# Two attention layers with experts on one core: where the product with the values stands in a slot, and where three weight loads are issued

## The chip, the cores and the metric

The kernel runs on one core of a Trainium2 chip. A core has five engines, each with a queue of its own that it works off in order: TensorE (PE, matrix products; its weight loads are listed apart as PEld), VectorE (DVE), ScalarE (ACT), GpSimd (POOL) and SyncE (SP), which here only issues transfers. They meet by semaphores. The metric is the device time of one launch in microseconds (us), lower is better.

## What is computed

Four sequences of 512 tokens with 128 features run through two layers. Cut to what matters:

```python
x = L0_attn_x                                   # (4, 512, 128), f32
xn = layernorm(x)
x = x + attention_0(xn) + swiglu_0(xn)          # 16 heads of 8; hidden 384, int weights / 127
xn = layernorm(x)
x = x + attention_1(xn, block_mask) + experts_1(xn)
# attention: softmax(q k^T / sqrt(8)) v, then a projection; the second one has a block mask
# experts: router -> best 2 of 8, capacity 1.25 * T / 8; each expert silu(x Wg) * (x Wu) @ Wd
```

## The kernel before

**Units and slots.** The work is eight units: four sequences in layer 0 (units 0 to 3), then the same four in layer 1 (units 4 to 7). A unit has 16 slots. A slot handles one block of 128 keys for four heads: two pairs of score products (`score_mms`, line 747; each pair is two products on the two halves of the array's rows), whose results ScalarE exponentiates (`exponential`, line 962) into `PT`, and one product with the values (`value_mms`, line 763, 4 products in f32 that the trace lists as 8 rows), one slot late: slot t does the product for slot t-1.

**Maxima.** Softmax needs the row maxima first. They are made 24 pairs ahead: a slot also has up to two pairs of score products for maxima (`max_mms`, line 732), which VectorE reduces (`read_max`, line 1114). There are 256 such pairs; 24 come before unit 0, so 116 slots carry two each, the last of them slot 3 of unit 7. The maxima are split (GpSimd), transposed (PE, line 739), copied to `mT` (ScalarE, line 955) and sent into rows of `QO` by SyncE (`max_rows`, line 444), for the slots 0 to 7 and 8 to 15 of a unit apart.

**PSUM.** Banks 0 to 5 form three pairs of banks. Scores, maxima, gate products and expert products take them in turn (`take_pair`): a job waits until the job three places before it in that row has been read. In a slot with maxima and nothing else the row is: score pair 0, maxima 0, score pair 1, maxima 1. So maxima 1 waits for the exponential of score pair 0 of the same slot, maxima 0 of the next slot for the exponential of score pair 1, and each score pair for VectorE's reduction of an earlier maximum. Bank 6 collects the product with the values, bank 7 is for everything else.

**Side work.** At the end of a slot PE does what is due besides: gate and up products of layer 0 (slots 9 to 11 of units 0 to 3, lines 785 and 786), expert work (two jobs a slot from slot 4 of unit 6 on, lines 792, 802, 803, 810), and `side_mms`: transposes (lines 687, 771, 777, 739), projections (line 693 and, for the values, 699 or 704), router and rank products. In slot 6 the projection of the output of the unit before is in two halves (`out_mms`, lines 822 and 825): the first between score pair 0 and score pair 1, the second at the slot's end. The first waits until `mT` was copied, since both use bank 7.

**ScalarE's row.** In each slot: exponential of pair 0, then most of the copies, then the exponential of pair 1, then `output_copy` (slots 0 and 8, line 968) or the tanh of gates (line 978) or an expert's result (line 994). `exponential` e waits for the product with the values of two slots before (`pv_done`), since `PT` has four buffers.

**SyncE's row.** Everything above issues from one queue, written out by hand: first loads, row constants, then `loads` (line 1370), the last three of which are the experts' weights `eg`, `eu` and `ed` of 1 MB each; then `sync_unit` for each unit. `loads` all count on one semaphore, `loaded`, on which the mask table (GpSimd, unit 0) and the expert products wait.

Of the kernel before, what the change touches and what calls it, by code (L numbers as in the profile page):

```python
# [12 lines left out]
P = 128  # L13
# [4 lines left out]
def build(nc, x, wq, wk, wv, bq, bk, bv, wo, bo, wg_T, wu_T, wd_T, src_blocks, tgt_blocks, router_T, eg_T, eu_T,  # L18
# [33 lines left out]
    with ExitStack() as ctx:  # L52
# [3 lines left out]
        def sem(name):  # L56
            return ctx.enter_context(nc.semaphore(name))
# [20 lines left out]
        w_router = sb("w_router", [P, E])  # L78
# [88 lines left out]
        emptied = sem("emptied")  # L167
        empty_ready = sem("empty_ready")
        loaded = sem("loaded")
        x_loaded = [sem(f"x_loaded{b}") for b in range(B)]  # L170
        zeros = sem("zeros")
        consts = sem("consts")
# [84 lines left out]
        def layer(u):  # L257
            return u // B
# [129 lines left out]
        def operand_writes(sp, p, side):  # L388
            if p >= 2 and side == 0:
                sp.wait_ge(qk_rows[(p - 2) % 3], reads_of(p - 2))  # L390
                if p == 2:
                    for landed in first_rows:
                        sp.wait_ge(landed, 16 * 4)
            for i in range(3):
                sp.wait_ge(part_ready[side], 3 * p + i + 1)
                a, z, step = SLOTS[i][side]
                dst = z_dram[p % 2][side].rearrange("s m t -> m s t")[:, a:z:step, :]
                n = len(range(a, z, step))
                sp.dma_start(dst, part[i][:, side, :].unsqueeze(1).to_broadcast([P, n, S])).then_inc(
                    z_written[side], 16)  # L400
# [46 lines left out]
        def sync_unit(sp, u):  # L447
            p, n = u + 2, u + 1
            if u == U - 2:
                for e in range(2):  # L450
                    load_places(sp, e)
                load_meta(sp)
                for e in range(2, 4):
                    load_places(sp, e)
            max_rows(sp, u, 1)
            if p < U:
                operand_writes(sp, p, 0)
                operand_writes(sp, p, 1)
                if layer(p) == 0:
                    operand_reads_0(sp, p)  # L460
                else:
                    operand_reads_1(sp, p, 0)
            if u == U - 2:
                for e in range(4, 7):
                    load_places(sp, e)
            if n < U:
                max_rows(sp, n, 0)
            if u == U - 2:
                load_places(sp, 7)
            if p < U and layer(p) == 1:  # L470
                operand_reads_1(sp, p, 1)
            if u < 2:
                empty_places(sp, u)
# [321 lines left out]
        def gate_up_1(pe, g):  # L795

            e, i, c = g // 4, g % 4 // 2, g % 2
            pe.wait_ge(loaded, N_LOAD)
            pe.wait_ge(places_ready, e + 1)
            pair = take_pair(pe, "gate1", g)  # L800
            cols, x_T = slice(i * P, (i + 1) * P), places_T[e % 2][:, c * HALF:(c + 1) * HALF]
            pe.matmul(ps[:, 2 * pair, 0:HALF], eg[:, e, cols], x_T, start=True, stop=True).then_inc(gate_ps[1], 1)  # L802
            pe.matmul(ps[:, 2 * pair + 1, 0:HALF], eu[:, e, cols], x_T, start=True, stop=True).then_inc(up_ps[1], 1)  # L803
# [95 lines left out]
        def tensor_unit(pe, u):  # L899
            if u < 3:  # L900
                pe.wait_ge(rows_set[u], 16 * N_ROW_DMAS)
            pe.wait_ge(m_rows[0], 16 * M_DMAS * (u + 1))
            for slot in range(SLOTS_U):
                if slot == 8:
                    pe.wait_ge(m_rows[1], 16 * M_DMAS * (u + 1))
                maxima = pairs_at(u, slot)
                score_mms(pe, u, slot, 0)
                if maxima:
                    max_mms(pe, maxima[0])
                if u > 0 or slot > 0:  # L910
                    value_mms(pe, SLOTS_U * u + slot - 1)
                if slot == 6 and u >= 1:
                    pe.wait_ge(mT_ready, 2 * u + 2)
                    out_mms(pe, u - 1, (0, 1))
                score_mms(pe, u, slot, 1)
                if maxima:
                    max_mms(pe, maxima[1])
                if gate_at(u, slot) is not None:
                    gate_up_0(pe, gate_at(u, slot))
                for kind, n in expert_work_at(u, slot):  # L920
                    if kind == "places":
                        places_mms(pe, n)
                    elif kind == "gate1":
                        gate_up_1(pe, n)
                    else:
                        expert_out(pe, n)
                side_mms(pe, u, slot)
# [282 lines left out]
        def last_vector(dve):  # L1210
            normalize_out(dve, U - 1, 1)
            for b in range(B):
# [13 lines left out]
                 (w_v[1][:], wv[1]),  # L1226
                 *((b_v1[32 * c:32 * c + 32], bv[1][None, 32 * c:32 * c + 32].to_broadcast([32, 32])) for c in range(4)),
                 (w_proj[1][:], wo[1]), (b_proj[1][:], bo[1][None, :].to_broadcast([P, D])),
                 (w_router[:], router_T), (eg[:], eg_T), (eu[:], eu_T),
                 (ed[:], ed_T.rearrange("e (b p) d -> p e b d", p=P))]  # L1230
        N_LOAD, N_FIRST = 16 * len(loads), 16 * len(first_loads)

        def load_x(sp, b):
            sp.dma_start(xs[b][:], x[b].rearrange("(t p) d -> p t d", p=P)).then_inc(x_loaded[b], 16)
# [276 lines left out]
```

## Time and profile before

| | us |
|---|---|
| median of 3 runs | 543.98 (542.29 to 545.46) |
| profiled execution, device time | 544.03 |
| its span (first to last instruction) | 542.0 |
| PE busy | 454.8 (84%) |
| VectorE busy | 400.5 (74%) |
| ScalarE busy | 328.8 (61%) |
| GpSimd busy | 262.5 (48%) |
| mean granted clock of TensorE | 0.95 of 2.4 GHz |

The device time is the span and 2.0 us around it. PE is the busiest engine and has 53% of the chain that ended last; VectorE has 18%, ScalarE 10%. PE idles 87.2 us in all, of which 26.9 us lie before unit 0 begins at 49.96 us and 17.1 us behind 513.55 us, in the last four slots and the end.

Two products of a pair run on different rows of the array at once, so a pair of score products shows 0.39 us while the next one may start 0.22 us after it.

### The profile page before, as it was taken

Reading aid. Unit: us, or ns where it says so; the run is one execution under the profiler, and the core shown is the slowest. Engines: PE = TensorE matmul, PEld = TensorE weight load, DVE = VectorE, ACT = ScalarE, POOL = GpSimd, SP = SyncE. Lnnn points to the kernel's source line nnn. Section 1 sums busy time; section 2 is a strip of 40 time slices with the busy share of each in tenths; the row PEclk is TensorE's granted clock in tenths of the full one; section 3 lists DMA queues with packets and bytes.
Section 4 is the critical chain, followed back from the end, with each engine's and each line's share of the span. In section 5 each row is a group of like instructions: output and inputs, shape, how many; then the busy total and the mean of one; then the engine's idle time right before and its main releaser. Section 6 shows DMA issues by size and latency. Waiting matters only on the chain.

```text
span 542.0 us, 9302 instructions
## 1 busy us (share of the span) xinstructions
PE 454.8 (84%) x3394; PEld 169.4 (31%) x3394; DVE 400.5 (74%) x538; ACT 328.8 (61%) x422; POOL 262.5 (48%) x499
## 2 busy tenths in 40 slices
PE   3456979889988999899989898987899999999952
PEld 1101213224322433242312431221245453455511
DVE  5699778886998699869887798789876777623204
ACT  2102666776677667656676577777766567667560
POOL 6861263724425562886378657884201233163240
PEclk9755889999999999999999999999999999999995
DMA  3896596244511360626252645174731111010018
GB/s 82 238 230 89 89 343 106 93 163 146 90 43 61 118 62 4 66 72 127 25 52 39 157 43 56 41 160 68 109 52 32 45 50 50 4 44 25 21 47 219
DMA packets 143742, 48.27 MB, mean 89 GB/s; under 512 B 109890, under 2 KB 139090, under 8 KB 142866
## 3 DMA queue, kind: packets, MB, share of 16 engines
q1 hardware_dynamic: 141394, 42.93, 38.1%
q0 software_dynamic: 2304, 4.76, 2.6%
q8 instruction: 27, 0.44, 0.3%
q14 instruction: 17, 0.14, 0.1%
HBM read 22.81 MB, written 23.14 MB: 85 GB/s over the span
## 4 chain that ended last, share of the span: by engine, by line
PE 53%; DVE 18%; issue 10%; ACT 10%; DMA 4%; SPq 4%; POOL 1%; POOLq 0%; ACTq 0%; DVEq 0%
PE ps L763 14%; DVE mx L1114 11%; PE ps L747 9%; PE ps L732 7%; ACT PT L962 6%; PE ps L802 3%; PE ps L810 3%; PE ps L785 2%; PE ps L803 2%; SPq L433 2%; PE ps L693 2%; PE ps L825 2%; PE ps L822 2%; PE ps L786 1%; DVE th L1135 1%
## 5 line engine op out<-in xcount | busy, mean ns | idle before, releaser
L1114 DVE TENSOR_REDUCE mx<-ps 128x2 f32<-128x1024 f32 x256 | 309.4, 1223 | 73.1 <-PE ps L732 65.1
L962 ACT ACTIVATE PT<-ps 128x1024 f32<-128x1024 f32 x256 | 258.6, 1026 | 125.9 <-PE ps L747 116.5
L763 PE MATMUL ps<-PT,Vp 128*32 128x512 f32 x1024 | 138.1, 611 | 5.4 <-ACT PT L962 4.4
L732 PE MATMUL ps<-KO,QO 48*128 48x512 bf16 (+1 forms) x512 | 104.5, 406 | 39.7 <-ACT PT L962 22.6
L747 PE MATMUL ps<-QO,KO 59*128 59x512 bf16 x512 | 100.2, 390 | 3.8 <-DMA QO<-mT 2.5
L520 POOL DMA_INDIRECT y_tokens<-expert_io,meta x40 | 38.6, 964 | 71.5 <-ACT expert_io L994 48.5
L747 PEld LDWEIGHTS ps<-QO,KO 59*128 59x128 bf16 x512 | 24.6, 93 | 142.8 <-issue 87.9
L1135 DVE SCALAR_TENSOR_TENSOR th<-th,ps 128x320 f32<-128x320 f32 (+1 forms) x44 | 23.8, 541 | 35.2 <-ACT th L978 29.4
L732 PEld LDWEIGHTS ps<-KO,QO 48*128 48x128 bf16 (+1 forms) x512 | 25.6, 96 | 70.9 <-ACT PT L962 38.6
L545 POOL CAST mp<-mx 128x32 bf16<-128x32 f32 x16 | 3.4, 214 | 82.9 <-DVE mx L1114 78.7
L509 POOL DMA_INDIRECT x_places<-xe,place_i x32 | 31.9, 995 | 22.3 <-ACT PT L962 15.2
L763 PEld LDWEIGHTS ps<-PT,Vp 128*32 128x32 f32 x1024 | 20.4, 108 | 45.7 <-issue 39.7
L978 ACT ACTIVATE th<-ps 128x320 f32<-128x320 f32 (+1 forms) x44 | 21.1, 487 | 12.0 <-PE ps L802 5.8
L802 PE MATMUL ps<-expert_io,eg 128*128 128x320 f32 x64 | 24.4, 462 | 2.1 <-ACT expert_io L994 0.6
L1150 DVE SCALAR_TENSOR_TENSOR h_all<-th,ps 128x320 f32<-128x320 f32 (+1 forms) x44 | 23.8, 541 | 1.5
L955 ACT COPY mT<-ps 24x512 bf16<-24x512 bf16 x16 | 9.0, 562 | 26.1 <-PE ps L739 26.1
L492 POOL TENSOR_SCALAR xe<-xs,mv,rstd 128x128 f32<-128x128 f32 x28 | 22.2, 802 | 0.8
L994 ACT ACTIVATE expert_io<-ps,meta 128x128 f32<-128x128 f32 x40 | 11.2, 372 | 18.6 <-PE ps L810 18.6
L803 PE MATMUL ps<-expert_io,eu 128*128 128x320 f32 x64 | 22.4, 432 | 0.0
L810 PE MATMUL ps<-ed,h_all 128*128 128x128 f32 x160 | 19.4, 276 | 1.2 <-DVE h_all L1150 1.2
L810 PEld LDWEIGHTS ps<-ed,h_all 128*128 128x128 f32 x160 | 18.9, 192 | 3.0 <-DVE h_all L1150 1.7
L1120 DVE RECIPROCAL rden<-ps 128x32 f32<-128x32 f32 x16 | 5.6, 349 | 16.3 <-PE ps L771 16.3
(166 smaller groups left out, 475.1 us busy)
## 6 DMA issues: line engine op xcount, KB each, us to landing
z<-part SPq DMA_DIRECT2D x16, 384.0 KB
z<-part SPq DMA_DIRECT2D x16, 256.0 KB
QO<-z SPq DMA_DIRECT2D x64, 48.0 KB
KO<-z SPq DMA_DIRECT2D x64, 48.0 KB
x_places<-expert_io SPq DMA_DIRECT2D x2, 1300.0 KB, 7.4
expert_io<-x_places SPq DMA_DIRECT2D x8, 320.0 KB, 3.5
QO<-z SPq DMA_DIRECT2D x6, 384.0 KB
KO<-z SPq DMA_DIRECT2D x6, 384.0 KB
```

The lines of the kernel that those rows point to most:

```text
L509: pool.indirect_dma_start(out=x_places[:], out_offset=bass.IndirectOffsetOnAxis(ap=place_i[:, b, t, k:k + 1], axis=0), in_=xe[p % 2][:, t, ...
L520: pool.indirect_dma_start(out=y_tokens[:], out_offset=bass.IndirectOffsetOnAxis(ap=meta[:].bitcast(I32)[:, e, j, 0:1], axis=0), in_=y_sb[e ...
L732: mm = pe.matmul(ps[:, 2 * pair + half, :], rows_of(QO[u % 3], half, 2 * s + jj, rows, (qt, qt + 1)), rows_of(KO[u % 3], half, 2 * s + jj, ...
L747: mm = pe.matmul(ps[:, 2 * pair + half, :], rows_of(KO[u % 3], half, 2 * s + jj, ROWS, (k, k + 1)), rows_of(QO[u % 3], half, 2 * s + jj, R ...
L763: last = pe.matmul(ps[32 * g:32 * g + 32, PV_BANK, :], Vp[u % 2][:, k, head(s, g), :], PT[:, (2 * t + g % 2) % 4, g // 2, :], start=(s % 2 ...
L802: pe.matmul(ps[:, 2 * pair, 0:HALF], eg[:, e, cols], x_T, start=True, stop=True).then_inc(gate_ps[1], 1)
L803: pe.matmul(ps[:, 2 * pair + 1, 0:HALF], eu[:, e, cols], x_T, start=True, stop=True).then_inc(up_ps[1], 1)
L810: last = pe.matmul(across(pair, j * P, (j + 1) * P), h1_T[:, e % 2, i, j * P:(j + 1) * P], ed[:, e, i, :], start=(i == 0), stop=(i == EB - 1))
L962: act.activation(PT[:, e % 4], ps[:, 2 * pair:2 * pair + 2, :], ACT.Exp).then_inc(exp_done, 1)
L1114: dve.tensor_reduce(mx[:, a, qt, col:col + 5:4], ps[:, 2 * pair:2 * pair + 2, :], AX_X, ALU.max, negate=True).then_inc(max_read, 1)
L1135: dve.scalar_tensor_tensor(out=t, in0=t, scalar=1.0, in1=ps[:, bank, 0:n], op0=ALU.add, op1=ALU.mult).then_inc(gate_done[L], 1)
L1150: dve.scalar_tensor_tensor(out=dst, in0=t, scalar=0.5, in1=ps[:, bank + 1, 0:n], op0=ALU.mult, op1=ALU.mult).then_inc(h_ready[L], 1)
```

## The change

Two things. In `tensor_unit`, the product with the values moves from between maxima 0 and score pair 1 to behind maxima 1, ahead of the gate, expert and side work. Where a slot has no maxima it moves behind score pair 1. Nothing else in PE's row moves, and no other engine's row but SyncE's. In SyncE's row, the loads of `eg` and `eu` move from the end of the first loads to unit 0, behind the rows for its second half and the operand writes for unit 2; the load of `ed` moves to the same place in unit 1. They get a semaphore of their own, on which the expert products now wait.

```diff
@@ sync_unit
                 operand_writes(sp, p, 0)
                 operand_writes(sp, p, 1)
+                if u < 2:
+                    for dst, src in expert_loads[0:2] if u == 0 else expert_loads[2:3]:
+                        sp.dma_start(dst, src).then_inc(experts_loaded, 16)
                 if layer(p) == 0:
                     operand_reads_0(sp, p)
@@ gate_up_1
-            pe.wait_ge(loaded, N_LOAD)
+            pe.wait_ge(experts_loaded, N_EXPERT)
@@ tensor_unit
                 score_mms(pe, u, slot, 0)
                 if maxima:
                     max_mms(pe, maxima[0])
-                if u > 0 or slot > 0:
-                    value_mms(pe, SLOTS_U * u + slot - 1)
                 if slot == 6 and u >= 1:
                     pe.wait_ge(mT_ready, 2 * u + 2)
                     out_mms(pe, u - 1, (0, 1))
                 score_mms(pe, u, slot, 1)
                 if maxima:
                     max_mms(pe, maxima[1])
+                if u > 0 or slot > 0:
+                    value_mms(pe, SLOTS_U * u + slot - 1)
                 if gate_at(u, slot) is not None:
                     gate_up_0(pe, gate_at(u, slot))
@@ loads
-                 (w_router[:], router_T), (eg[:], eg_T), (eu[:], eu_T),
-                 (ed[:], ed_T.rearrange("e (b p) d -> p e b d", p=P))]
+                 (w_router[:], router_T)]
+        expert_loads = [(eg[:], eg_T), (eu[:], eu_T), (ed[:], ed_T.rearrange("e (b p) d -> p e b d", p=P))]
```

PE's row in slot 4 of unit 2, which ends with a key projection as side work. L747 are score pairs, L732 maxima, L763 the product with the values; `exp_done` is a wait for an exponential, `max_read` for a reduction. Before:

```order
L747 MATMUL ps<-QO,KO 128x512 [waits max_read]
L747 MATMUL ps<-QO,KO 128x512
L732 MATMUL ps<-KO,QO 128x512 [waits exp_done]
L732 MATMUL ps<-KO,QO 128x512
L763 MATMUL ps<-PT,Vp 32x512 [waits exp_done]
L763 MATMUL ps<-PT,Vp 32x512 x3
L747 MATMUL ps<-QO,KO 128x512 [waits max_read]
L747 MATMUL ps<-QO,KO 128x512
L732 MATMUL ps<-KO,QO 128x512 [waits exp_done]
L732 MATMUL ps<-KO,QO 128x512
L693 MATMUL ps<-xnT,w_k 128x512 [waits xnT_ready,onT_ready,qk_f_ready]
```

The same slot in the changed kernel, whose lines are numbered 4 higher (L751 scores, L736 maxima, L767 values, L697 projection):

```order
L751 MATMUL ps<-QO,KO 128x512 [waits max_read]
L751 MATMUL ps<-QO,KO 128x512
L736 MATMUL ps<-KO,QO 128x512 [waits exp_done]
L736 MATMUL ps<-KO,QO 128x512
L751 MATMUL ps<-QO,KO 128x512 [waits max_read]
L751 MATMUL ps<-QO,KO 128x512
L736 MATMUL ps<-KO,QO 128x512 [waits exp_done]
L736 MATMUL ps<-KO,QO 128x512
L767 MATMUL ps<-PT,Vp 32x512 [waits exp_done]
L767 MATMUL ps<-PT,Vp 32x512 x3
L697 MATMUL ps<-xnT,w_k 128x512 [waits xnT_ready,onT_ready,qk_f_ready]
```

Between score pair 0 and maxima 1, which waits for that pair's exponential, the product with the values stood before; now only maxima 0 and score pair 1 do. The value product stands between maxima 1 and the side work.

PE's row in slot 6 of unit 3, from score pair 0 to the second half of the output projection. Before:

```order
L747 MATMUL ps<-QO,KO 128x512 [waits max_read]
L747 MATMUL ps<-QO,KO 128x512
L732 MATMUL ps<-KO,QO 128x512 [waits exp_done]
L732 MATMUL ps<-KO,QO 128x512
L763 MATMUL ps<-PT,Vp 32x512 [waits exp_done]
L763 MATMUL ps<-PT,Vp 32x512 x3
L822 MATMUL ps<-w_proj,o_T 128x128 [waits h_ready0,onT_ready,mT_ready]
L825 MATMUL ps<-wd,h_all 128x128 x3
```

In the changed kernel:

```order
L751 MATMUL ps<-QO,KO 128x512 [waits max_read]
L751 MATMUL ps<-QO,KO 128x512
L736 MATMUL ps<-KO,QO 128x512 [waits exp_done]
L736 MATMUL ps<-KO,QO 128x512
L826 MATMUL ps<-w_proj,o_T 128x128 [waits h_ready0,onT_ready,mT_ready]
L829 MATMUL ps<-wd,h_all 128x128 x3
```

The value product went from ahead of the wait for `mT` to behind score pair 1 and maxima 1.

SyncE's row at the start of unit 0 in the changed kernel; L445 are the maxima rows, L400 the operand writes for unit 2, L411 its operand reads:

```order
L1374 DMA w_router<-in_router_T 128x8
L445 DMA QO<-mT 3x4x512 x2
L400 DMA z_0<-part 128x3x512
L400 DMA z_0<-part 128x2x512
L400 DMA z_0<-part 128x512
L400 DMA z_1<-part 128x3x512
L400 DMA z_1<-part 128x2x512
L400 DMA z_1<-part 128x512
L462 DMA eg<-in_eg_T 128x2048
L462 DMA eu<-in_eu_T 128x2048
L411 DMA QO<-z_0 48x4096
```

Before, `eg`, `eu` and `ed` stood between `w_router` and the maxima rows. Now `eg` and `eu` are behind the operand writes, ahead of the operand reads of unit 2.

## Rows read from the trace of the kernel before

**Rows 1.** Windows, units 0 to 7: length, busy PE PEld DVE ACT POOL, clock, DMA, GB/s

```profile
49.96:105.93 55.97, 48.71 (x292) 12.62 (x293) 46.11 (x52) 36.30 (x42) 25.04 (x56) 0.90 0.57 139
105.93:161.74 55.81, 51.23 (x346) 17.49 (x345) 46.50 (x57) 38.07 (x45) 19.76 (x41) 1.00 0.42 120
161.74:217.53 55.79, 51.51 (x348) 17.55 (x346) 46.51 (x57) 38.31 (x46) 29.39 (x68) 1.00 0.30 66
217.53:275.17 57.64, 52.20 (x468) 18.21 (x466) 46.90 (x63) 38.23 (x46) 37.56 (x76) 1.00 0.43 69
275.17:328.51 53.34, 47.24 (x456) 16.34 (x454) 43.03 (x57) 36.32 (x43) 37.53 (x76) 1.00 0.46 74
328.51:377.97 49.46, 42.92 (x420) 12.12 (x419) 41.62 (x47) 35.72 (x41) 36.77 (x71) 1.00 0.51 85
377.97:452.17 74.20, 69.02 (x564) 31.88 (x563) 56.91 (x78) 49.55 (x74) 17.75 (x25) 1.00 0.31 57
452.17:513.55 61.38, 57.59 (x365) 31.58 (x365) 27.85 (x49) 39.65 (x68) 20.30 (x25) 1.00 0.09 30
```

**Rows 2.** Timeline of PE and ACT, a quiet slot: start, length, operation [idle before]

```profile
106.96 0.39 PE L732 MATMUL ps<-KO,QO 48*128 48x512 bf16 x2 [0.63 <-ACT PT L962]
107.28 1.07 PE L763 MATMUL ps<-PT,Vp 128*32 128x512 f32 x8
108.28 0.39 PE L747 MATMUL ps<-QO,KO 59*128 59x512 bf16 x2
108.50 0.38 PE L732 MATMUL ps<-KO,QO 48*128 48x512 bf16 x2
...
109.79 0.39 PE L732 MATMUL ps<-KO,QO 48*128 48x512 bf16 x2 [0.69 <-ACT PT L962]
...
108.71 1.02 ACT L962 ACTIVATE PT<-ps 128x1024 f32<-128x1024 f32 x1 [0.89 <-PE ps L747]
```

**Rows 3.** Timeline of PE, unit 2: a slot's begin, then one with a projection

```profile
168.23 0.39 PE L747 MATMUL ps<-QO,KO 59*128 59x512 bf16 x2
168.62 0.39 PE L732 MATMUL ps<-KO,QO 48*128 48x512 bf16 x2
...
176.85 0.38 PE L732 MATMUL ps<-KO,QO 48*128 48x512 bf16 x2
177.16 1.13 PE L693 MATMUL ps<-xnT,w_k 128*128 128x512 f32 x2
178.22 0.39 PE L747 MATMUL ps<-QO,KO 59*128 59x512 bf16 x2
```

**Rows 4.** Timeline, slot 6 of unit 3, engines as named

```profile
237.35 0.39 PE L747 MATMUL ps<-QO,KO 59*128 59x512 bf16 x2
...
238.74 0.56 ACT L955 COPY mT<-ps 24x512 bf16<-24x512 bf16 x1
...
239.36 0.49 PE L822 MATMUL ps<-w_proj,o_T 128*128 128x128 f32 x2
```

**Rows 5.** Waits of PE over the whole span: in total, times, longest

```profile
PE ps L732 <- ACT PT L962: 22.6, 40, 0.8
```

**Rows 6.** Timeline of SP and PE, the start of slot 8 of unit 0

```profile
71.42 2.67 SPq L444 DMA_DIRECT2D QO<-mT  x2
...
77.39 0.39 PE L747 MATMUL ps<-QO,KO 59*128 59x512 bf16 x2 [2.55 <-DMA QO<-mT]
...
77.97 1.93 PE L763 MATMUL ps<-PT,Vp 128*32 128x512 f32 x8
```

**Rows 7.** Timeline of PE and ACT, unit 6, the slot behind an expert's output

```profile
447.02 0.39 PE L747 MATMUL ps<-QO,KO 59*128 59x512 bf16 x2
...
449.50 0.39 PE L732 MATMUL ps<-KO,QO 56*128 56x512 bf16 x2 [0.53 <-ACT PT L962]
...
447.12 1.40 ACT L994 ACTIVATE expert_io<-ps,meta 128x128 f32<-128x128 f32 x5 [2.33 <-PE ps L810]
```

**Rows 8.** Timeline of POOL, the first of the last seven sends of expert results

```profile
516.24 0.96 POOL L520 DMA_INDIRECT y_tokens<-expert_io,meta  x1 [5.31 <-ACT PT L962]
```

More of the change, by code:

```diff
@@ L169, in build @@
         loaded = sem("loaded")
+        experts_loaded = sem("experts_loaded")
         x_loaded = [sem(f"x_loaded{b}") for b in range(B)]
@@ L1228, in build @@
                  (w_proj[1][:], wo[1]), (b_proj[1][:], bo[1][None, :].to_broadcast([P, D])),
-                 (w_router[:], router_T), (eg[:], eg_T), (eu[:], eu_T),
-                 (ed[:], ed_T.rearrange("e (b p) d -> p e b d", p=P))]
-        N_LOAD, N_FIRST = 16 * len(loads), 16 * len(first_loads)
+                 (w_router[:], router_T)]
+        expert_loads = [(eg[:], eg_T), (eu[:], eu_T), (ed[:], ed_T.rearrange("e (b p) d -> p e b d", p=P))]
+        N_LOAD, N_EXPERT, N_FIRST = 16 * len(loads), 16 * len(expert_loads), 16 * len(first_loads)
         def load_x(sp, b):
```

## The prediction

> **What bounds the kernel now.** I read first the busy time of each unit, then PE's timeline slot by slot, then its waits. In units 1 to 7 PE is busy 87 to 94% of the time [rows 1], so it is the engine that sets the pace, but not everywhere. Two kinds of slot must be told apart, and the reader should see them in the timeline.
>
> A quiet slot has two score pairs, two pairs of maxima and the product with the values, and nothing else. There PE waits. From one maxima 0 to the next [rows 2]: the value product starts 0.32 us later, score pair 1 1.00 us after that, its exponential 0.43 us later and takes 1.02 us, and 0.06 us on the next maxima 0 starts, since it needs the banks that this exponential reads: 0.32 + 1.00 + 0.43 + 1.02 + 0.06 = 2.83 us, which is 109.79 - 106.96. PE idles 0.63 to 0.69 us of it. So a quiet slot is bound by a ring through PE and ScalarE.
>
> A slot with side work is bound by PE alone. Without waits, PE's own pitches are 0.22 (score pair 0), 0.32 (maxima 0), 1.00 (values), 0.22 (score pair 1) and 0.31 (maxima 1, followed by something of another kind), 2.07 us in all, plus the side work. In the slot with the key projection maxima 1 to the next score pair is 1.37 us = 0.31 + 1.06 [rows 3], so the slot takes 3.13 us, and the next maxima 0 finds its exponential done: the side work stands in the time in which PE would have waited. That is how most waits are hidden now, and PE's waits of maxima for exponentials add up to only 22.6 us in 40 places [rows 5].
>
> **The value product moved, slot by slot.** Two rings run through each slot: score pair 0 and its exponential to maxima 1 of the same slot, and score pair 1 and its exponential to maxima 0 of the next slot. Before, the first had the value product inside it (0.22 + 0.32 + 1.00 + 0.22 = 1.76 us of PE work from score pair 0 to maxima 1, against 0.43 + 1.02 + 0.06 = 1.51 us that the exponential needs), and the second had the side work. So each had its cover. Now both covers are in the second ring. In the first there are score pair 0, maxima 0 and score pair 1: 0.22 + 0.22 + 0.39 = 0.83 us until PE is empty, then 0.68 us of idling until 1.51.
>
> - *Quiet slot, after:* 1.51 (score pair 0 to maxima 1) + 0.32 + 1.00 = 2.83 us. The same as now: the wait goes from maxima 0 to maxima 1. Nothing won, nothing lost.
> - *Slot with side work s, after:* 2.83 + s, against 2.07 + s. It costs 0.76 us, of which 0.68 is idling. It can't be hidden by the side work, since that comes behind the wait.
>
> I count 116 slots with maxima. Slot 6 of units 1 to 6 is apart, which leaves 110: 81 with side work (9, 11, 12, 12, 11, 9, 13 and 4 in units 0 to 7) and 29 quiet ones.
>
> Slot 6: the first half of the output projection waits for `mT`, whose copy is behind the exponential of score pair 0. It starts 2.01 us after score pair 0 [rows 4]; the value product lies inside that. After, the start is the same 2.01 us, PE has 0.22 + 0.38 = 0.60 us of work in it and idles 1.4 us, and the value product's 1.00 us comes later. In units 1 to 7, where there is such a projection, that is 1.4 us of idling each, 9.8 us in the sum below; maxima 1 then has no wait.
>
> Behind an expert's output ScalarE first copies the result, 1.40 us [rows 7], then does the exponential of score pair 0, and maxima 1 starts 2.48 us after score pair 0 (449.50 against 447.02), still waiting for ScalarE although the value product stands before it. Against 1.51 that is 0.97 more in four such slots with maxima: 3.9 us.
>
> **The loads moved.** In unit 0 PE stands still for 2.55 us at slot 8 for the maxima rows, issued at 71.42 behind 3 MB of weights, and runs the next value product in 1.93 instead of 1.07 us [rows 2, 6]. Without the loads ahead of it that wait has between nothing and 2.5 us left; I take nothing, as two slots, 5.66 us, lie between the copy's slot and the wait. That is 2.5 us, and 0.9 for the product at the lower clock. The new places cost nothing: the issues stand behind operand writes for unit 2 that PE needs only from slot 4 of unit 1, over ten slots later, so 2 MB ahead of the operand reads (and `ed` ahead of those for unit 3) are covered; without that cover it would be again 2.5 us at a time. The mask table's loads come earlier, which nobody waits for.
>
> **The sum**, by PE's time. Busy in units 0 to 7: 48.7 + 51.2 + 51.5 + 52.2 + 47.2 + 42.9 + 69.0 + 57.6 = 420.3 us [rows 1], less 0.9 for the clock. Idling and transitions that the new order makes: 81 x 0.76 = 61.6, 29 x 0.69 = 20.0 (already there in some, but not in busy time), slot 6 9.8, experts 3.9. Waits that stay: 3.8 in unit 7 (61.38 - 57.59), where slots 4 to 15 have no maxima and the value product's place changes no ring, and some 1.5 of unit 0's first slots (of 7.3 in all, between nothing and 4.7 without the 2.55). Together 520.0 us, against 463.6 now (513.55 - 49.96): +56.4. All other present waits of PE in these units (the reductions, the normalized output) fall behind the value product and are gone in this sum.
>
> From that comes off what counts as busy but is a wait: where maxima 0 follows 0.39 instead of 0.22 us behind its score pair, as at 168.23 [rows 3], no idle time shows, because the rows overlap. PE's timeline has 77 late followers of this kind; 48 of them are not in quiet slots, each some 0.15 us: -7. The head before 49.96 is untouched. The tail isn't moved by PE: the last seven sends of GpSimd start at 516.24 [rows 8] behind an exponential that follows an expert's result copy, and the end hangs on them; quiet slots of unit 7 may get shorter by some tenths and win nothing. So **+49 us: 544 + 49 = 593 us**, from the profiled execution's 544.03, which the median of 543.98 equals.
>
> **A rule against the change.** At full clock the quiet slots of rows 2 idle 0.69 us each, and the granted clock is 1.00 in units 1 to 7 [rows 1]; after the 2.55 us wait it was at the lower level (1.93 us for a value product) [rows 6]. The Trainium skill, TensorE: Matmul & The Clock Gate, "A second HAM failure mode: psum-queue depth-cycling", tells of a kernel that went round its PSUM banks, made PE idle briefly between groups, and had its clock swing between both levels. By that rule the new waits would cost more than their length; it is a rival below. The trace speaks against it so far, with 0.69 us idling in slot after slot at 1.00.
>
> **Rivals.**
>
> 1. *The clock falls.* The longest new waits are slot 6's 1.4 us. If each sent the clock to 1.2 GHz for a slot, as the 2.55 us did, it would cost some 0.9 us for the value product and as much for the rest: 7 x 1.8 = 13 us more, 606 us; if also slots with 0.68 us did, far more (0.9 us per value product in half of 110 slots, 50 us: 643). For it: more idling than now. Against it: rows 1 and 2, as told. Chance 0.08.
> 2. *The loss is smaller, since other engines pace the side-work slots.* VectorE is busy 81 to 84% in units 1 to 5 [rows 1]. Where a gate's two products on VectorE or the reductions already hold PE, the new idling takes the place of that waiting. If a third more of the 61.6 us fell on such places, it would be 573 us. For it: units 0 to 5 idle 4 to 7 us each now. Against it: those waits are already out of the sum. Chance 0.08.
> 3. *Faster.* The mechanism: only the old waits vanish (22.6 at maxima 0, 3.4 at the load) and maxima 1 doesn't wait, because its exponential is early enough: 544 - 26 = 518 us. It decides at the point where PE has 1.51 us of work between score pair 0 and maxima 1; it has 0.83. The banks would have to be taken in another turn than the row says. Chance 0.02.
> 4. *Nothing changes but the load.* If the side work slipped into the wait after all, as it does now, every slot would be like the quiet one: 541 us, the 3.4 us won. PE works its row in order, which speaks against it. Chance 0.02.
>
> **How the numbers follow.** The forecast, 593 us with its own 580 to 603, has 0.80. Its low end is slot pitches by hand, 63.1 us for unit 2 instead of 64.1, and rival 2 in part; its high end the sum without the 7 us and with the load's 2.5 us back. For 8 in 10, with a little of rivals 1 and 2: 578 to 605. Faster by over 0.5% (2.7 us, about what a measurement of this kernel can tell from no change) 0.03, within 0.5% 0.02, slower 0.95.
>
> **What would show it.** Right: maxima rows waiting for exponentials in over 100 places, about 0.68 us each, some 75 us in all, now at the second pair of maxima; the slot with the key projection 3.9 instead of 3.1 us; unit 2 about 63 to 64 us, unit 7 only 3 to 5 us longer; the output projection in slot 6 behind 1.4 us of idling; no wait for `QO<-mT` at slot 8 of unit 0; the clock at 1.00 in units 1 to 6. Wrong: side-work slots of their old length, or value products at 1.93 us in the middle of the run.

## The result, and the profile after

The changed kernel takes 584.01 us (median of 4 runs, 583.26 to 587.78), beside 544.16 us for the kernel before on the same chip (4 runs): a ratio of 1.0749, 95% interval 1.0693 to 1.0805. It is 40 us slower, where 49 were forecast; 584 lies inside the forecast's own range of 580 to 603.

The profiled execution took 583.26 us, with a span of 580.8 us against 542.0. PE is busy 452.5 us (78%), where it was 454.8 (84%), so all of the new time is idling. PE's share of the chain that ended last rose from 53 to 58%, ScalarE's from 10 to 20%.

Windows of the changed kernel, units 0 to 7 in the first eight rows, then the last four slots of unit 7 and the end, which the row of unit 7 leaves out as [rows 1] does (length, then busy time of PE, PEld, DVE, ACT and POOL, granted clock, DMA share, GB/s):

```profile
49.83:107.46 57.63, 47.38 (x292) 13.32 (x292) 46.69 (x53) 36.76 (x42) 26.33 (x61) 0.94 0.49 120
107.46:169.97 62.51, 51.17 (x349) 18.11 (x346) 46.48 (x58) 37.26 (x44) 19.12 (x38) 1.00 0.44 125
169.97:232.64 62.67, 51.33 (x350) 18.22 (x347) 46.58 (x58) 37.43 (x45) 29.30 (x68) 1.00 0.27 55
232.64:295.71 63.07, 51.73 (x470) 18.84 (x467) 46.96 (x64) 37.43 (x45) 37.43 (x76) 1.00 0.39 63
295.71:353.21 57.50, 45.87 (x458) 16.64 (x454) 42.96 (x58) 35.64 (x42) 37.38 (x76) 1.00 0.43 68
353.21:406.65 53.44, 42.01 (x423) 12.62 (x420) 41.54 (x48) 35.52 (x40) 36.22 (x69) 1.00 0.47 79
406.65:488.40 81.75, 69.46 (x565) 32.49 (x561) 56.05 (x78) 48.33 (x73) 17.53 (x24) 1.00 0.28 52
488.40:552.42 64.02, 57.21 (x364) 31.36 (x363) 27.68 (x49) 39.57 (x68) 20.10 (x24) 1.00 0.08 27
552.42:580.80 28.38, 11.93 (x73) 4.53 (x72) 6.89 (x12) 10.30 (x15) 6.70 (x7) 0.73 0.46 127
```

Set against [rows 1], the eight units are 1.7, 6.7, 6.9, 5.4, 4.2, 4.0, 7.6 and 2.6 us longer, 39.0 in all. The head (49.83 against 49.96) and the last stretch (28.38 against 28.45) hardly changed. Unit 0, which has the load's gain in it, and unit 7, where the maxima end with slot 3, lose least; unit 6, with maxima and expert work in its slots, most. PE idles 86.4 us in the units (the lengths less the busy times) where it was 43.2. The clock stands at 1.00 from unit 1 to 7.

The waits of PE in the changed kernel (what waited, for whom, total us, times, longest):

```profile
PE ps L736 <- ACT PT L966: 57.4, 92, 0.9
PE ps L736 <- DVE mx L1118: 10.8, 21, 0.6
PE ps L826 <- ACT mT L959: 9.7, 7, 1.6
PE ps L751 <- DVE h_all L1154: 8.6, 19, 0.7
...
PE ps L751 <- DVE mx L1118: 3.6, 7, 0.7
...
PE ps L751 <- ACT expert_io L998: 2.4, 3, 0.9
```

The first row answers to [rows 5]: 57.4 us in 92 places where it was 22.6 in 40. The second is not new: it stands in the trace of before with the same 10.8 us in 21 places, all but one of them ahead of unit 0. The two rows on L751 with `h_all` and `expert_io` are score pairs that wait for a gate product's reader or for an expert result's copy.

PE's timeline in unit 2 of the changed kernel, from the second pair of scores of slot 4 to the value product of slot 6; 190.61 is score pair 0 of slot 6, 194.56 its score pair 1 (start, length, operation, idle before it and its releaser):

```profile
184.15 0.38 PE L751 MATMUL ps<-QO,KO 59*128 59x512 bf16 x2
185.21 0.39 PE L736 MATMUL ps<-KO,QO 48*128 48x512 bf16 x2 [0.68 <-ACT PT L966]
185.53 1.07 PE L767 MATMUL ps<-PT,Vp 128*32 128x512 f32 x8
186.53 1.13 PE L697 MATMUL ps<-xnT,w_k 128*128 128x512 f32 x2
187.58 0.39 PE L751 MATMUL ps<-QO,KO 59*128 59x512 bf16 x2
...
190.61 0.39 PE L751 MATMUL ps<-QO,KO 59*128 59x512 bf16 x2
...
192.58 0.49 PE L826 MATMUL ps<-w_proj,o_T 128*128 128x128 f32 x2 [1.35 <-ACT mT L959]
192.90 0.83 PE L829 MATMUL ps<-wd,h_all 128*128 128x128 f32 x6
...
194.56 0.39 PE L751 MATMUL ps<-QO,KO 59*128 59x512 bf16 x2
...
195.10 1.06 PE L767 MATMUL ps<-PT,Vp 128*32 128x512 f32 x8
```

This is the mechanism in three readings. At 185.21 the second maxima wait 0.68 us for the exponential of score pair 0. Behind them stand the value product (1.00 us) and the key projection (1.05 us), which could have filled that wait and come too late for it. And in slot 6 the projection starts 1.97 us after score pair 0 (192.58 against 190.61), as it did before [rows 4], but now with 1.35 us of idling in front, and the value product still to come at 195.10.

ScalarE in the same slot 6: the copy of `mT`, which releases the projection, stands right behind the exponential.

```profile
191.04 1.02 ACT L966 ACTIVATE PT<-ps 128x1024 f32<-128x1024 f32 x1 [0.52 <-PE ps L751]
191.97 0.56 ACT L959 COPY mT<-ps 24x512 bf16<-24x512 bf16 x1
```

### The profile page after: what moved, and what is told of

Its sections match the earlier page's. It is cut to its first block, busy times and chain, and to the rows that moved or that the text cites. A ratio compares the mean times of both kernels' runs of the same rounds, so it can differ in the third digit from the quotient of the medians.

```text
span 580.8 us, 9302 instructions
## 1 busy us (share of the span) xinstructions
PE 452.5 (78%) x3394; PEld 174.6 (30%) x3394; DVE 400.1 (69%) x538; ACT 324.2 (56%) x422; POOL 261.6 (45%) x499
## 4 chain that ended last, share of the span: by engine, by line
PE 58%; ACT 20%; DVE 10%; issue 7%; DMA 2%; POOL 1%; SPq 1%; POOLq 0%; ACTq 0%; DVEq 0%
PE ps L767 20%; ACT PT L966 16%; PE ps L736 7%; PE ps L751 7%; DVE mx L1118 5%; PE ps L814 3%; PE ps L806 3%; PE ps L807 2%; PE ps L789 2%; PE ps L697 2%; PE ps L829 2%; PE ps L826 2%; DMA h_all<-y_tokens 1%; PE ps L790 1%; DVE th L1139 1%
## 5 line engine op out<-in xcount | busy, mean ns | idle before, releaser
L966 ACT ACTIVATE PT<-ps 128x1024 f32<-128x1024 f32 x256 | 254.9, 1027 | 132.5 <-PE ps L751 124.0
L736 PE MATMUL ps<-KO,QO 48*128 48x512 bf16 (+1 forms) x512 | 104.5, 406 | 73.7 <-ACT PT L966 57.4
L767 PE MATMUL ps<-PT,Vp 128*32 128x512 f32 x1024 | 137.1, 607 | 1.7 <-issue 1.0
L751 PE MATMUL ps<-QO,KO 59*128 59x512 bf16 x512 | 98.4, 387 | 16.8 <-DVE h_all L1154 8.6
L736 PEld LDWEIGHTS ps<-KO,QO 48*128 48x128 bf16 (+1 forms) x512 | 25.2, 95 | 127.0 <-ACT PT L966 97.5
L751 PEld LDWEIGHTS ps<-QO,KO 59*128 59x128 bf16 x512 | 24.2, 93 | 100.7 <-issue 33.5
L767 PEld LDWEIGHTS ps<-PT,Vp 128*32 128x32 f32 x1024 | 20.2, 108 | 34.9 <-issue 33.1
L826 PE MATMUL ps<-w_proj,o_T 128*128 128x128 f32 x64 | 13.1, 314 | 10.9 <-ACT mT L959 9.7
```

Of the source, the lines that this page charges most:

```text
L736: mm = pe.matmul(ps[:, 2 * pair + half, :], rows_of(QO[u % 3], half, 2 * s + jj, rows, (qt, qt + 1)), rows_of(KO[u % 3], half, 2 * s + jj, ...
L751: mm = pe.matmul(ps[:, 2 * pair + half, :], rows_of(KO[u % 3], half, 2 * s + jj, ROWS, (k, k + 1)), rows_of(QO[u % 3], half, 2 * s + jj, R ...
L767: last = pe.matmul(ps[32 * g:32 * g + 32, PV_BANK, :], Vp[u % 2][:, k, head(s, g), :], PT[:, (2 * t + g % 2) % 4, g // 2, :], start=(s % 2 ...
L826: last = pe.matmul(ps[:, SIDE, tok], o_T[:, tok], w_proj[L][:], start=True, stop=(L == 1))
L966: act.activation(PT[:, e % 4], ps[:, 2 * pair:2 * pair + 2, :], ACT.Exp).then_inc(exp_done, 1)
```

## The experiments

The kernels ran in groups, each beside the kernel before. That measured 539.4 us in the first group (values alone, the loads alone for the first time, slot 6, early side work) and 543.8 to 544.3 us in the others, so each ratio is against the kernel before of its own group. The changed kernel, run again in the last group, gave 583.95 us, ratio 1.0732 [1.0706, 1.0757], with units within 0.6 us of those above. It was not run in the first group.

### The two parts apart

Values alone, the loads left in their old place (against the kernel before):

```diff
                 if maxima:
                     max_mms(pe, maxima[0])
-                if u > 0 or slot > 0:
-                    value_mms(pe, SLOTS_U * u + slot - 1)
...
                 if maxima:
                     max_mms(pe, maxima[1])
+                if u > 0 or slot > 0:
+                    value_mms(pe, SLOTS_U * u + slot - 1)
```

> The value product at its new place, all loads at their old one. My theory (the exponential of score pair 0 has lost its cover, 0.68 us of idling before maxima 1 in every slot with side work): nearly the whole loss, and the stall of unit 0 at slot 8 as before or a little less, since that slot comes later: 584 to 588 us. Rival (the loads' new place costs part of the 40 us, for instance operand reads behind 2 MB): under 575 us.

It measured 583.45 us, ratio 1.0811 [1.0768, 1.0855], span 580.5. Units 1 to 6 are 62.52, 62.67, 62.88, 57.35, 53.10 and 81.76 us, those of the changed kernel within 0.4 us. The whole loss is the value product's. The issue of the maxima rows and the start of slot 8 of unit 0, timelines of SyncE and PE of this kernel:

```profile
74.09 1.62 SPq L444 DMA_DIRECT2D QO<-mT  x2
...
78.07 0.39 PE L747 MATMUL ps<-QO,KO 59*128 59x512 bf16 x2 [0.20 <-DMA QO<-mT]
```

Against 2.55 us in [rows 6] only 0.20 us of the wait for the maxima rows is left although the loads stand ahead of them. The expectation, a stall as before or a little less, missed this. The late value products put the copy of `mT` off, so that the rows are issued at 74.09 instead of 71.42, while the first of the three weight loads is issued at nearly the same time (65.37, before 65.00). From their issue to the score pair it takes 3.98 us instead of 5.97. PE's own work in that stretch grew by less, from 3.42 to 3.78 us.

Loads alone (against the changed kernel, the value product put back between maxima 0 and score pair 1):

```diff
                 if maxima:
                     max_mms(pe, maxima[0])
+                if u > 0 or slot > 0:
+                    value_mms(pe, SLOTS_U * u + slot - 1)
...
                     max_mms(pe, maxima[1])
-                if u > 0 or slot > 0:
-                    value_mms(pe, SLOTS_U * u + slot - 1)
```

> The value product at its old place, the loads at their new one. My theory: the stall of 2.55 us at slot 8 of unit 0 and the slow clock behind it vanish, all else as before: 540 to 541 us. Rival (the loads collide with unit 2's operands): 544 us or more, with a wait of PE for a transfer of z in unit 1.

It measured 535.92 us, ratio 0.9937 [0.9921, 0.9954]. Run again in the last group it gave 541.54, ratio 0.9949 [0.9935, 0.9962]:

> The loads alone again, beside the kernel with late value products in unit 7. My theory: 0.992 to 0.995 of the kernel before. Rival (the gain of the first time was the chip's): above 0.998.

Both say some 3 us, as worked out: slots 7 and 8 of unit 0 take 2.87 and 3.97 us instead of 5.54 and 4.70 in the kernel before. At slot 8 the score pair no longer waits, and the value product runs in 1.07 us; PE's timeline of the first of the two kernels, slot 8 of unit 0:

```profile
75.87 0.39 PE L751 MATMUL ps<-QO,KO 59*128 59x512 bf16 x2
76.89 0.39 PE L736 MATMUL ps<-KO,QO 48*128 48x512 bf16 x2 [0.63 <-ACT PT L966]
77.21 1.07 PE L767 MATMUL ps<-PT,Vp 128*32 128x512 f32 x8
```

So in time the parts don't add up. Alone, the loads' new place is worth 3 us. With late value products the traces leave it some 0.3: slot 7 of unit 0 takes 3.09 us in the kernel with the values alone and 2.83 in the changed one, and of the slots behind it only five differ, by 1.3 us together and in the other direction (slot 8 of units 3 to 5 and slots 5 and 10 of unit 7). The ratios seem to say otherwise, 1.0811 against 1.0749 and 1.0732, as if the loads had won 3 to 4 us here too. But they stand on kernels before of 539.4 us and of 544.2 and 544.3; the kernels themselves took 583.5, 584.0 and 584.0.

### Slot 6

The value product of slot 6 of units 1 to 7 put back ahead of the wait for `mT`, all else as changed:

```diff
+                if slot == 6 and u >= 1:
+                    value_mms(pe, SLOTS_U * u + slot - 1)
                 if slot == 6 and u >= 1:
                     pe.wait_ge(mT_ready, 2 * u + 2)
...
-                if u > 0 or slot > 0:
+                if (u > 0 or slot > 0) and not (slot == 6 and u >= 1):
                     value_mms(pe, SLOTS_U * u + slot - 1)
```

> The changed kernel with slot 6 of units 1 to 7 in the old order (values ahead of the output projection). My theory: the value product fills the wait for mT again, 1.0 us in each of seven units, 577 us; slot 6 of unit 2 falls from 7.47 to 6.47 us. Rival (the time in slot 6 is given back later, since VectorE catches up there): less than half of that.

It measured 576.07 us, ratio 1.0673 [1.0635, 1.0712], span 573.3, which is 7.5 us below the changed kernel's: 1.0 us for each of the seven projections. The slot takes 6.47 us instead of 7.47, its length before. The waits of PE in this kernel have 2.7 us where the changed kernel has 9.7:

```profile
PE ps L826 <- ACT mT L961: 2.7, 7, 0.6
```

### Half an exponential

Four kernels leave out half of one exponential in each slot from slot 2 of unit 0 on (it then takes 0.60 instead of 1.02 us, and the results are not right): that of score pair 0 or that of score pair 1, in the changed kernel and in the kernel before. If the ring through pair 0 sets the changed kernel's pace, only pair 0 may matter there.

```diff
             pair = pair_of("score", e)
-            act.activation(PT[:, e % 4], ps[:, 2 * pair:2 * pair + 2, :], ACT.Exp).then_inc(exp_done, 1)
+            halves = 1 if e >= 4 and e % 2 == 0 else 2
+            act.activation(PT[:, e % 4, 0:halves], ps[:, 2 * pair:2 * pair + halves, :], ACT.Exp).then_inc(exp_done, 1)
```

Pair 0, changed kernel:

> The changed kernel, in which the exponential of score pair 0 handles only one of its two banks (the rest of the probabilities is left out), so that it takes about 0.6 instead of 1.02 us. My theory (it sets the time of every slot with maxima): 0.42 us off 81 slots, 0.35 off 29 quiet ones where VectorE's two reductions of 1.22 us are next, and 0.42 at each mT: 584 - 45 = 539 us, give or take 5. Rival (VectorE or PE's own work sets the slot): under 10 us off.

It measured 546.15 us, ratio 1.0052 [1.0022, 1.0083], span 543.4: 37.4 us less than the changed kernel, where 45 were expected. In the timeline of PE, unit 1 of this kernel, the wait of maxima 1 has shrunk from 0.68 to 0.26 us:

```profile
109.15 0.39 PE L736 MATMUL ps<-KO,QO 48*128 48x512 bf16 x2 [0.26 <-ACT PT L967]
109.47 1.06 PE L767 MATMUL ps<-PT,Vp 128*32 128x512 f32 x8
110.78 1.13 PE L697 MATMUL ps<-xnT,w_q 128*128 128x512 f32 x2 [0.25 <-DVE o_nat L1133]
```

Quiet slots take 2.40 instead of 2.83 us, the full 0.43. Where the gain is smaller another wait came next: in slot 2 the query projection now waits for the normalized output (110.78 above; 3.77 instead of 3.88 us), and slot 10 stays at 5.23, since its score pair 1 waits for a gate product's reader. These two slots fall short of 0.43 by 5.4 us in all the units; the rest is spread over others, slot 8 above all (1.8 us).

Pair 1, changed kernel (`e % 2 == 1` in the diff):

> The changed kernel, in which the exponential of score pair 1 handles only one bank. My theory (it is covered by the value product and the side work): within 2 us of the changed kernel, 582 to 584 us. Rival (ScalarE's total work counts): as much off as with pair 0.

587.69 us, ratio 1.0817 [1.0775, 1.086]: no gain at all from halving 126 exponentials, and quiet slots of 2.83 us as before. It is 4 us slower than the changed kernel, which was not expected; it ran only twice, and one of the four times of the changed kernel was 587.78. Slot 4 of units 4 and 5 has 4.80 and 4.83 instead of 3.88 us. In unit 4 of this kernel maxima 1 waits there for the exponential of score pair 0, and that one starts 1.35 us after its scores (311.46) instead of 0.43:

```profile
311.46 0.39 PE L751 MATMUL ps<-QO,KO 59*128 59x512 bf16 x2
...
313.89 0.39 PE L736 MATMUL ps<-KO,QO 56*128 56x512 bf16 x2 [1.61 <-ACT PT L967]
...
312.81 1.02 ACT L967 ACTIVATE PT<-ps 128x1024 f32<-128x1024 f32 x1 [2.25 <-PE ps L751]
```

This 0.92 us is what the slot is longer by. In the same stretch a reduction of VectorE waits for GpSimd, where the split of the maxima stands behind the scatter of tokens to their experts:

```profile
312.92 1.23 DVE L1119 TENSOR_REDUCE mx<-ps 128x2 f32<-128x1024 f32 x1 [1.71 <-POOL mp L555]
```

But PE does not wait for that reduction in this slot. What held the exponential is not in the rows; with other values in the attention the routing is another too, and whether that matters was not tried.

Pair 0, kernel before:

> The kernel before, with the exponential of score pair 0 on one bank only. My theory (there it has the value product as cover): only the copies of mT come earlier, 0 to 4 us off, 540 to 544 us. Rival (the exponential of pair 0 always counts): 20 us off or more.

539.40 us, ratio 0.9934 [0.9892, 0.9976]. Units 1 and 2 take 55.69 us each, where they took 55.81 and 55.79. The 37 us that the same edit gives behind the change are 4 here: with the value product in its old place that exponential had its cover.

Pair 1, kernel before:

> The kernel before, with the exponential of score pair 1 on one bank only. My theory (it sets the quiet slots there, 29 with maxima and part of some more): 0.35 us each and more where a short side work leaves a wait, 10 to 16 us off, 528 to 534 us. Rival (no effect, as PE is the bound everywhere): under 3 us.

537.67 us, ratio 0.9897 [0.9817, 0.9976], where 528 to 534 was expected. The ring through pair 1 is the one that the kernel before waits on: units 1 and 2 take 54.20 and 54.16, 1.6 us less each, and the waits of maxima for exponentials fall from 22.6 to 5.3 us. But slot 4 of unit 3 takes 6.63 instead of 3.48 us (maxima 0 idles 1.73 us for no releaser that the profile names, and the value product behind it takes 1.85 us), maxima rows are waited for in seven places, 5.3 us, where it was one, and units 3 to 7 together are 1.0 us longer. The direction holds, the size was missed. It ran only twice.

The two pairs of kernels show the rings changing places: before, half of exponential 1 helps the quiet slots and half of exponential 0 doesn't; after, exponential 0 gives 37 us and exponential 1 none.

### Other orders of the row

The value product between score pair 1 and maxima 1, inside the first ring again but behind both score pairs (loads as changed):

```diff
                 score_mms(pe, u, slot, 1)
-                if maxima:
-                    max_mms(pe, maxima[1])
                 if u > 0 or slot > 0:
                     value_mms(pe, SLOTS_U * u + slot - 1)
+                if maxima:
+                    max_mms(pe, maxima[1])
```

> The changed kernel with the value product one place earlier, between score pair 1 and maxima 1. My theory: it is cover for both exponentials there (0.22 + 0.22 + 0.32 + 1.00 = 1.76 us from score pair 0 to maxima 1, and as much and the side work from score pair 1 to the next maxima 0), so PE doesn't wait for ScalarE; but from maxima 1 to the next score pair 1, which waits for its reduction (0.43 + 1.22 + 0.06 = 1.71 us), PE has only 0.66 us and the side work. So a quiet slot takes 0.32 + 1.00 + 1.71 = 3.03 us and waits for VectorE, a slot with side work s the larger of 3.03 and 2.07 + s: 545 us, 540 to 552. Rival (any delay of the value product costs as the changed kernel does): over 570 us.

It measured 567.88 us, ratio 1.0436 [1.0398, 1.0474], where 545 was expected; that is nearer to the rival's 570. Part of what was expected came: waits of maxima for exponentials are nearly gone, and quiet slots take 3.03 us. The waits of PE in this kernel:

```profile
PE ps L751 <- DVE mx L1118: 27.8, 44, 1.3
PE ps L826 <- ACT mT L959: 11.2, 7, 4.7
...
PE ps L736 <- ACT PT L966: 2.6, 10, 0.7
```

Score pair 1 now waits for VectorE in 44 places: it needs the banks of an earlier maxima pair and has only score pair 0 and maxima 0 ahead of it, as maxima 1 had in the changed kernel. What was overlooked were the slots in which score pair 1 or the projection has a wait of its own. Unit 2 is 3.1 us longer than before: 1.10 in slot 6 (7.57 us, the value product behind the wait for `mT`), 0.44, 0.43 and 0.48 in slots 10, 11 and 12, 0.40 in slot 8. Unit 7 adds something else, in slot 6:

```profile
505.64 1.22 PE L826 MATMUL ps<-w_proj,o_T 128*128 128x128 f32 x4 [4.67 <-ACT mT L959]
...
507.33 1.94 PE L767 MATMUL ps<-PT,Vp 128*32 128x512 f32 x8
```

ScalarE's own row there shows what held it (last section). So the prediction's account of the ring holds, but score pair 1 has such a ring too, through VectorE.

Side work of slots 1 and 10, and of slot 8 in units 0 and 1, in the new gap, between score pair 1 and maxima 1:

```diff
                 score_mms(pe, u, slot, 1)
+                early = maxima and (slot in (1, 10) or slot == 8 and u < 2)
+                if early:
+                    side_mms(pe, u, slot)
...
-                side_mms(pe, u, slot)
+                if not early:
+                    side_mms(pe, u, slot)
```

> The changed kernel, in which the transposes of slots 1 and 10 (and the value projection of slot 8 in units 0 and 1) stand between score pair 1 and maxima 1 instead of behind the value product. My theory: work there is cover for the exponential of score pair 0, so each of these 15 or so transposes takes some 0.55 us off its slot and the two projections 0.68 each: 8 to 10 us less than the changed kernel, 574 to 576 us; slot 1 falls from 3.61 to about 3.0 us. Rival (changing between the kinds of products is what costs, whatever waits): no gain, since there are as many changes.

It measured 582.83 us, ratio 1.0794 [1.0754, 1.0833]; its span of 580.6 equals that of the values alone, 580.5. The expectation was missed by 7 us. Slot 1 did as worked out: 3.02 instead of 3.61 us in six units, 3.5 us won, and slot 8 of units 0 and 1 won 0.75 and 0.35. Slot 10 lost 0.25 in units 0 to 3, since its score pair 1 already waited for a gate's reader and maxima 1 for nothing (score pairs wait 11.8 us on `h_all` in 21 places, 8.6 in 19 in the changed kernel), and slot 9 behind an early slot 8 lost 0.19. And in slot 2 of unit 7, where the changed kernel takes 5.70 us, this one takes 7.78. PE's timeline there, of this kernel:

```profile
499.78 0.39 PE L751 MATMUL ps<-QO,KO 59*128 59x512 bf16 x2 [0.95 <-ACT expert_io L1002]
500.69 0.39 PE L736 MATMUL ps<-KO,QO 56*128 56x512 bf16 x2 [0.52 <-ACT PT L970]
501.01 1.70 PE L767 MATMUL ps<-PT,Vp 128*32 128x512 f32 x8
```

The value product takes 1.70 instead of 1.07 us: the granted clock is at its lower level, 1.2 GHz, from 501.31 to 504.72. So filling the gap works where the gap is, in slot 1, which bears out the mechanism; the rest of the gain was claimed where no gap was.

Value product late only where a slot has no maxima (not slot 6), loads as changed:

```diff
+                late = not maxima and slot != 6
+                if (u > 0 or slot > 0) and not late:
+                    value_mms(pe, SLOTS_U * u + slot - 1)
...
-                if u > 0 or slot > 0:
+                if late:
                     value_mms(pe, SLOTS_U * u + slot - 1)
```

> Loads at their new place; the value product at its old place in all slots with maxima and in slot 6 of unit 7, and behind score pair 1 in the other slots of unit 7, where no maxima wait. My theory: there the order makes no new wait, the last four slots shrink (1.83 instead of 2.51 us each) but the end hangs on GpSimd's sends: the end comes within 1 us of the kernel with the loads alone, at 0.992 to 0.995 of the kernel before. Rival (the late value product costs by itself, wherever it stands): 2 us or more longer than with the loads alone.

540.96 us, ratio 0.9939 [0.9925, 0.9952]; the loads alone beside it gave 0.9949 [0.9935, 0.9962]. Unit 7's last slots do get shorter (2.83 and 1.82 us instead of 3.06 and 2.51), and the time does not, by what the runs can tell: the last seven sends of GpSimd start at 512.67 us, with the loads alone at 512.37, and the end hangs on them, as the prediction had it. This kernel and the loads alone beat both the kernel before and the changed one; between the two the runs can't tell.

The changed kernel once more:

> The changed kernel itself, on the same chip as the other two, so that its two parts can be added up. My theory: the parts add up (1.0811 with the values alone, 0.9937 with the loads alone): 1.0811 - 0.0063 = 1.075 of the kernel before. Rival (the loads' new place costs when the value product is late): 1.08 or more.

583.95 us, as told at the head of this section, so the new order costs the same beside this kernel before as beside the first. The ratio expected from adding up the parts, 1.075, was met, but by two ratios that stand on different times of the kernel before, as told under the two parts; it does not show that the parts add up.

## Why the prediction came out as it did

**The ring, right.** Maxima 1 idles 0.68 us in place after place, in side-work slots too; the slot with the key projection takes 3.88 us (predicted 3.9), slot 5 of unit 2 3.03 us; quiet slots stay at 2.83. The half exponentials show that it is the pair 0 ring, and not merely that time was lost.

**The number of places and their sum, too high.** The forecast was over 100 places and some 75 us of maxima waiting for exponentials. They do so in 92, 57.4 us. Only with the score pairs that wait for a gate's reader, a reduction or an expert's result (8.6 + 3.6 + 2.4, of which 1.1 stood before too), which the prediction did not name, is it 72.0 us in 121 places. Where score pair 1 itself has to wait, it and maxima 1 share one stretch of time, which the sum had counted as the full 0.76 beside the other wait. Of the four places behind an expert's output that were priced at 0.97 us more each, 3.9 in all, three have such a wait, at score pair 1, and 1.9 us beyond the ring's own 0.68; the fourth has none.

**Slot 6, right.** 9.8 us were predicted, 9.7 us in seven places stand in the waits; putting the value product back took 7.5 us off, 1.0 to 1.1 for each projection.

**The loads, right in the sum, but not all theirs.** The stall of 2.55 us and the slow value product are gone, as the sum has it, and alone the loads are worth 3 us. What the prediction didn't see is that the late value products remove that stall by themselves: with the old loads the values alone show 0.20 us of it and take the same time as both parts together. The sum is right there for the two parts together, since it takes the stall off once.

**Units and tail.** Unit 2 was to take 63 to 64 us and takes 62.67; unit 7 was to be 3 to 5 us longer and is 2.6, both just under what was said; no `QO<-mT` wait is left; the clock is 1.00 in units 1 to 7, so rival 1 did not happen; the tail is the same to 0.1 us, GpSimd's seven last sends having moved with the rest. They start at 555.11, against 516.24 in [rows 8]:

```profile
555.11 0.95 POOL L524 DMA_INDIRECT y_tokens<-expert_io,meta  x1 [5.08 <-ACT PT L966]
```

**The terms that were too large.** Taken by PE's time in the eight units, the sum was 520.0 us, less 7 for waits hidden in busy time: 513. It measured 502.6, 10.4 less. Two terms make it:

- *Busy time, 2.7 us.* The sum has 425.9 us busy (420.3 - 0.9, and 0.08 in each of 81 slots), less the 7. It measured 416.2. Where rows of matmuls overlap, waits up to 0.17 us each hide in the busy time of before (0.39 less 0.22). If all of the 2.7 is of this kind, they came to 9.7 instead of 7 us; no run measures them apart.
- *Idling, 7.7 us.* Of 94.1 us of idling in the sum 86.4 came. Unit 0 has 2.2 less: in its first two slots, for the most part at the lower clock, PE's own work is longer and maxima 1 waits for no exponential. Unit 7 has 2.1 less, half of it in its slots 0 to 3, where score pair 1 has a wait of its own and only one maxima pair waits for its exponential (0.52 us), and half in the 3.8 us of waits said to stay: some 2.7 did (0.62, 0.88, 1.03 and small ones), the others fell behind the value product. Unit 6 has 2.2 less; there the shared waits told above are most frequent, and by its timeline 1.3 of it are places behind an expert's output, though no run parts them off. The rest, 1.2 us, is spread over the others.

The slot pitches by hand, which gave 63.1 us for unit 2 and were named as the low end, were nearer (62.67) than the sum from the window's busy time: a slot's length from pitches counts each wait once, while busy time of a pipelined engine has waits in it. Rival 2, a loss made smaller by other engines' pace, is in part what unit 6 shows: 2 us, not the 20 that it was priced at.

## What to carry to other kernels

Where jobs take turns on PSUM banks, write down for each job which reader it waits for, and how much work of the queue's own lies between that reader's input and the job: work that moves out of this stretch is lost as cover even if it stays in the same slot, and what stands behind the waiting instruction can't fill the gap. Price such a move slot by slot from pitches, and look for slots in which the moved job had another wait ahead of it, since these were the misses of the orders tried here. When two edits remove the same stall, their gains don't add.

## What the runs showed of the hardware that was not expected

**The clock's two sides.** 79 waits for exponentials of up to 0.9 us and seven for `mT` of up to 1.6 left the granted clock at 1.00 for units 1 to 7 of the changed kernel. With a hold of 4.67 us (the kernel with the value product ahead of maxima 1) the next value product took 1.94 us, and behind an idling of 1.73 us (the kernel before with half of exponential 1, slot 4 of unit 3) it took 1.85. The rule weighed in the prediction (the Trainium skill, TensorE: Matmul & The Clock Gate, "A second HAM failure mode: psum-queue depth-cycling") did not set in for the regular idling of 0.68 us a slot. In the kernel with early side work the value product of 501.01 took 1.70 us after waits of 0.95 and 0.52 close together, behind a slot with expert work. But the changed kernel has the same two waits twice in unit 6, at full clock; PE's timeline:

```profile
466.42 0.39 PE L751 MATMUL ps<-QO,KO 59*128 59x512 bf16 x2 [0.95 <-ACT expert_io L998]
467.34 0.39 PE L736 MATMUL ps<-KO,QO 56*128 56x512 bf16 x2 [0.52 <-ACT PT L966]
467.66 1.06 PE L767 MATMUL ps<-PT,Vp 128*32 128x512 f32 x8
```

So these waits alone are not what lowered the clock there, and what did stays open.

**ScalarE stood still for almost 4 us.** ScalarE's timeline of the kernel with the value product ahead of maxima 1, in slot 6 of unit 7:

```profile
503.47 0.77 ACT L982 ACTIVATE th<-ps 128x320 f32<-128x320 f32 x2 [3.85 <-remote]
```

The changed kernel has 3.88 us of the same kind ahead of `o_sb` at 565.11, in the tail, and 3.89 in the same place when run again; the traces of the kernel before, of the values alone and of the loads alone have none. "remote" names no instruction of the kernel, so what it is stays open.

**One kernel, two times 1% apart.** The kernel with the loads alone took 535.9 us in one group of runs and 541.5 in another, and the kernel before moved with it (539.4 and 544.3). The kernels with late values hardly moved: the values alone took 583.5 in the first group, the changed kernel 584.0 in the last. Part of the difference is in slot 5 of unit 4, and slot 8 of units 3, 4 and 5 has another 2.1 us. PE's timeline of the loads alone, first group:

```profile
288.29 0.39 PE L751 MATMUL ps<-QO,KO 59*128 59x512 bf16 x2
...
290.74 0.39 PE L751 MATMUL ps<-QO,KO 59*128 59x512 bf16 x2
```

and last group:

```profile
287.65 0.39 PE L751 MATMUL ps<-QO,KO 59*128 59x512 bf16 x2
288.77 0.39 PE L736 MATMUL ps<-KO,QO 56*128 56x512 bf16 x2 [0.74 <-ACT PT L966]
...
290.96 0.39 PE L751 MATMUL ps<-QO,KO 59*128 59x512 bf16 x2
```

The slot takes 2.45 us in the one, 3.31 in the other, where the exponential of score pair 1 of the slot ahead starts 1.65 us after its scores instead of 0.43. In the changed kernel the same slot takes 3.03 us. What holds that exponential is not in the rows, and it was not tried.
